# Mixture-of-experts layer with a domain adapter on one core: index records for SyncE, a hold on GpSimd's output operations, one power per layernorm

## The chip, the cores and the metric

The kernel runs on one core of a Trainium2 chip. The metric is the device time of one launch in microseconds (us), the median of several runs. TensorE does the matmuls, VectorE, ScalarE and GpSimd the elementwise work, and SyncE (SP) issues most of the DMAs.

## What is computed

128 sequences of 64 tokens with 256 features each go through two layers. Each sequence has an expert out of 8 and a domain out of 16.

```python
h = gelu(x @ Wi[e] + bi[e]); o = h @ Wo[e] + bo[e]        # 256 -> 1024 -> 256, e = itok_B_0_7
y = layernorm(o + x, 1e-12) * gamma[e] + beta[e]
a = gelu(y @ down_W.T + down_b)                            # 256 -> 64
a = where(valid, a @ expert_W[d].T + expert_b[d], a) + domain_emb[d]   # d = itok_B_0_15
out = layernorm(a @ up_W.T + up_b + y, 1e-5) * ln_gamma + ln_beta
```

## The kernel before

**Tiles.** A tile is two sequences of the same expert: 128 tokens. A sort on VectorE, TensorE and GpSimd in the first 15 us assigns the sequences to 136 slots, two per tile, so that there are 68 tiles, some with empty slots. It writes the indices that address the DMAs and the weights into the one row `idx`: for each slot the source (`IDX_SRC`) and the destination (`IDX_DST`), per tile the expert, for each of 64 weight chunks its place in HBM (`IDX_CHUNK`), and four numbers per step for TensorE. The engines load them into registers as they need them (`index`, `indices`).

**Precision.** Every f32 operand of a large product is split into a high and a low f16 part. ScalarE writes the high part (`x_hi`, `h_hi`, W's half), VectorE the low one (`x_lo` L723, `h_lo` L764, W's other half L727) as scaled value minus high part, and TensorE does three products (L918 to L920, L926 to L928).

**Steps.** The program is a software pipeline. Step i does, on the engines at the same time: the first product of tile i and, behind it, the second product of tile i-1 in eight parts j (TensorE), the first layernorm of tile i-2 (`r1`, `bn_stats`, `bn_aggr`, `z1`), the transposition of z1 between the fourth and fifth part of the second product (L959), the adapter's down product for tile i-3 and its up product and second layernorm for tile i-4, and the output of tile i-5. 73 steps in all; steps 0 to 7 are written out, the middle is a loop whose body holds 4 steps (8 on ScalarE and VectorE), the end is written out again. In the steps with weights one more weight chunk of 128 x 512 is loaded, split and stored, for a later expert.

**Every engine has its own queue in program order**, and engines meet at semaphores: `pe.wait_ge(z1_done, i - 1)` before the transposes, for example. What is written first on an engine runs first; a waiting instruction blocks everything behind it.

**VectorE's step:** r1 (L774, the product plus x, out of PSUM), its bn_stats (L777), r2 into yg (L783, out of PSUM), its bn_stats (L786), first bn_aggr (L788), low part of the adapter's activation `a1s` (L794), second bn_aggr (L797), the second half of h_lo for tile i-1, z1 (L805), y (L812), x_lo, the low part of a chunk, the first half of h_lo for tile i. `mv` holds mean and variance of both layernorms, `rs` their power -1/2.

**GpSimd's step:** for tile i-5 y times ln_gamma (L466) and plus ln_beta (L468); z1 times gamma into yg (L474); then one power for both layernorms of the step:

```python
pool.tensor_tensor(rs[:, both], mv[:, both, 1], neg_half[:, both], ALU.pow).then_inc(rs_done, 1)   # L484
```

and three small copies (L488, L494, L454) which gather gamma, the selection and the bias for ScalarE and TensorE.

**SP's step:** the chunk's index and the chunk for step i+2 (L253, L338), the sources of tiles i to i+2 and the transposed x of tile i+2 (L258, L322), the wait for `y_done`, the two destinations and two output DMAs (L258, L372), and x in its natural layout for tile i (L330). `x_T` and `y` have two buffers each.

Of the kernel before, what the change touches and what calls it, by code (L numbers as in the profile page):

```python
# [26 lines left out]
IDX_SRC, IDX_DST = 0, SLOTS  # L27

IDX_EXP = 2 * SLOTS + 3
IDX_CHUNK = IDX_EXP + TILES + 2  # L30

IDX_PE = IDX_CHUNK + CHUNKS
IDX_LEN = IDX_PE + 4 * STEPS


def build(nc, t):
# [4 lines left out]
    with ctx:  # L41
# [136 lines left out]
        CHUNK_READY, SRC_READY, TILE_READY, ALL_READY = 1, 2, 3, 4  # L178
# [45 lines left out]
        rs_done = sem("rs_done")  # L224
# [78 lines left out]
        def _(sp):  # L303
# [13 lines left out]

            def load_turned(b, i, parity):
# [23 lines left out]
            def load_first(chunks, of):  # L342
                for c, m in zip(chunks, of):
                    sp.dma_start(first_stage[m], t["w"][bass.ds(c * P, P), :]).then_inc(first_in[m], 16)

            chunks = indices(sp, IDX_CHUNK, FIRST_CHUNKS // 2, CHUNKS - 1)
            load_first([chunks[m] for m in FIRST_ORDER[:4]], FIRST_ORDER[:4])
            load_first(indices(sp, IDX_CHUNK + FIRST_CHUNKS // 2, FIRST_CHUNKS // 2, CHUNKS - 1), FIRST_ORDER[4:])
            sp.wait_ge(idx_ready, SRC_READY)
            b = [indices(sp, 2 * i + IDX_SRC, 2, B - 1) for i in range(2)]  # L350
            load_turned(b[1], 1, 1)
            for j in range(AHEAD):
                load_later(j, j % SLOTS_W)
# [6 lines left out]
            def step(i, parity, four, weights):  # L360
                if weights:
                    load_later(i + AHEAD, weights[2])

                if exists(i):
                    b = indices(sp, 2 * i + IDX_SRC, 6 if exists(i + 2) else 2, B - 1)
                if exists(i + 2):
                    load_turned(b[4:6], i + 2, parity)
                if exists(i - 5):
                    sp.wait_ge(y_done, i - 4)
                    to = indices(sp, 2 * i + (IDX_DST - 10), 2, SLOTS - 1)  # L370
                    for n in range(2):
# [705 lines left out]
```

## Time and profile before

| | us |
|---|---|
| median of 3 runs | 537.85 (537.72 to 538.39) |
| profiled execution | 537.86 |
| its span, first to last instruction | 535.9 |
| TensorE busy | 493.2 (92%) |
| VectorE busy | 423.7 (79%) |
| ScalarE busy | 381.8 (71%) |
| GpSimd busy | 315.0 (59%) |
| SP among the chain that ended last | 37% |

The span is the time between the first and last instruction of the core; a little lies around it. Busy shares are coverage: matmuls overlap each other, so TensorE's 92% does not say that 8% could be had. TensorE's granted clock is 1.00 of full speed in the whole tile loop. PE is TensorE, PEld its weight loads, DVE VectorE, ACT ScalarE, POOL GpSimd; a q behind it is the engine's own queue of instructions that compute nothing, such as issuing a DMA.

### The profile page before, as it was taken

The page shows a single profiled execution, that of the slowest core. Times are in us where ns is not written, and L with a number is a line of the kernel's source. Part 1 is how long each engine was busy: PE and PEld are TensorE (multiplying, and loading weights), DVE is VectorE, ACT ScalarE, POOL GpSimd, SP SyncE. Part 2 cuts the span into 40 slices and gives each one's busy share as a digit, 9 for nine tenths or more (in the row PEclk, how much of TensorE's full clock was granted, in tenths as well). Part 3 has the DMA queues.
Part 4 walks back from the last instruction along what each step waited for, and adds up shares of the span by engine and source line. Part 5 has one row for each costly group of instructions (what it writes and reads, how often), then busy time and mean ns, then how long its engine had stood idle before and what let it go on. Part 6 is the DMA issues. An engine that isn't in the chain of part 4 may idle for free.

```text
span 535.9 us, 19427 instructions
## 1 busy us (share of the span) xinstructions
PE 493.2 (92%) x5778; PEld 432.0 (81%) x5779; DVE 423.7 (79%) x935; ACT 381.8 (71%) x1099; POOL 315.0 (59%) x521
## 2 busy tenths in 40 slices
PE   5699999999999999999989999999999999999962
PEld 3489988888888878888878888888878888888951
DVE  6677888888888888788888888887888877677762
ACT  2688777787877777777778777787777876677741
POOL 5043666666656566565665566655666655555554
PEclk9799999999999999999999999999999999999995
DMA  4734333333333333323333333333333222222111
GB/s 115 245 95 103 87 91 94 79 91 89 93 93 80 87 92 89 92 78 90 91 90 91 84 91 87 90 90 87 87 88 89 63 64 58 61 62 56 46 32 29
DMA packets 70256, 45.83 MB, mean 86 GB/s; under 512 B 43969, under 2 KB 61778, under 8 KB 70098
## 3 DMA queue, kind: packets, MB, share of 16 engines
q1 hardware_dynamic: 69200, 45.25, 31.5%
q8 instruction: 15, 0.25, 0.2%
q10 hardware_dynamic: 1026, 0.21, 0.2%
q14 instruction: 15, 0.12, 0.1%
HBM read 36.51 MB, written 8.91 MB: 85 GB/s over the span
## 4 chain that ended last, share of the span: by engine, by line
SPq 37%; PE 35%; issue 11%; DVE 6%; POOL 4%; DMA 3%; ACT 2%; POOLq 1%; DVEq 0%; ACTq 0%
SPq L258 9%; SPq L322 8%; SPq L372 7%; SPq L330 7%; PE p_h L918 5%; PE p_h L919 4%; PE p_h L920 4%; PE p_o L928 4%; PE p_o L926 4%; PE p_o L927 4%; SPq L338 3%; PE p_d L937 2%; DMA x_T<-in_xT 2%; POOL rs L484 2%; PE p_t L959 2%
## 5 line engine op out<-in xcount | busy, mean ns | idle before, releaser
L918 PE MATMUL p_h<-x_hi,W 128*128 128x128 f16 x1088 | 194.0, 220 | 5.6 <-issue 5.3
L919 PE MATMUL p_h<-x_lo,W 128*128 128x128 f16 x1088 | 193.4, 220 | 0.0
L920 PE MATMUL p_h<-x_hi,W 128*128 128x128 f16 x1088 | 193.3, 220 | 0.0
L484 POOL TENSOR_TENSOR rs<-mv,neg_half 128x2 f32<-128x2 f32 (+1 forms) x70 | 67.6, 966 | 162.4 <-DVE mv L797 156.8
L581 ACT ACTIVATE h<-p_h,bi_tile 128x128 f32<-128x128 f32 x544 | 152.6, 362 | 0.4 <-PE p_h L920 0.4
L926 PE MATMUL p_o<-W,h_hi 128*128 x544 | 148.3, 273 | 0.0
L927 PE MATMUL p_o<-W,h_hi 128*128 x544 | 148.3, 273 | 0.0
L928 PE MATMUL p_o<-W,h_lo 128*128 x544 | 148.3, 273 | 0.0
L764 DVE SCALAR_TENSOR_TENSOR h_lo<-h,h_hi 128x512 f16<-128x512 f32 x136 | 124.5, 915 | 1.0 <-ACT h_hi L589 0.9
L918 PEld LDWEIGHTS p_h<-x_hi,W 128*128 x1088 | 106.7, 98 | 19.7 <-issue 18.3
L919 PEld LDWEIGHTS p_h<-x_lo,W 128*128 x1088 | 106.7, 98 | 1.5
L920 PEld LDWEIGHTS p_h<-x_hi,W 128*128 x1088 | 106.7, 98 | 0.0
L589 ACT ACTIVATE h_hi<-h 128x512 f16<-128x512 f32 x136 | 85.4, 628 | 2.2
L555 ACT ACTIVATE x_hi<-x_T 128x256 f16<-128x256 f32 x68 | 28.3, 416 | 72.5 <-DMA x_T<-in_xT 72.4
L474 POOL TENSOR_TENSOR yg<-z,g_t 128x256 f32<-128x256 f32 x68 | 73.2, 1076 | 2.5 <-DVE z L805 2.5
L468 POOL TENSOR_TENSOR y<-y,lnb 128x256 f32<-128x256 f32 x68 | 70.2, 1033 | 5.3
L466 POOL TENSOR_TENSOR y<-y,lng 128x256 f32<-128x256 f32 x68 | 56.6, 832 | 25.6 <-DVE y L812 25.6
L727 DVE SCALAR_TENSOR_TENSOR W<-stage,W 128x512 f32 (+1 forms) x56 | 66.5, 1187 | 0.1
L805 DVE TENSOR_SCALAR z<-r,mv,rs 128x256 f32<-128x256 f32 x68 | 32.2, 473 | 39.9 <-POOL rs L484 39.9
L621 ACT ACTIVATE yT<-p_t,gb_tile 128x128 f32<-128x128 f32 x136 | 54.8, 454 | 9.9 <-PE p_t L959 5.7
L928 PEld LDWEIGHTS p_o<-W,h_lo 128*128 128x128 f16 x544 | 53.2, 98 | 6.2
L927 PEld LDWEIGHTS p_o<-W,h_hi 128*128 128x128 f16 x544 | 53.2, 98 | 6.2
(153 smaller groups left out, 715.7 us busy)
## 6 DMA issues: line engine op xcount, KB each, us to landing
stage<-in_w SPq DMA_DIRECT2D x56, 256.0 KB, 2.6
x_nat<-in_x SPq DMA_DIRECT2D x136, 64.0 KB, 2.1
out<-y SPq DMA_DIRECT2D x136, 64.0 KB, 2.0
x_T<-in_xT SPq DMA_DIRECT2D x134, 64.0 KB, 2.2
W<-in_w SPq DMA_DIRECT2D x8, 256.0 KB, 4.1
g_t<-in_gamma SPq DMA_DIRECT2D x1, 1024.0 KB, 7.7
W<-in_expert_W SPq DMA_DIRECT2D x2, 128.0 KB, 3.0
upT<-in_up_W SPq DMA_DIRECT2D x2, 64.0 KB, 2.6
```

What stands on the lines that cost most here:

```text
L468: pool.tensor_tensor(last, last, lnb[:, :], ALU.add).then_inc(y_done, 1)
L474: pool.tensor_tensor(yg[:, 1 - parity, :], z1[:, :], g_t[:, bass.ds(e_third * D, D)], ALU.mult)\
L484: pool.tensor_tensor(rs[:, both], mv[:, both, 1], neg_half[:, both], ALU.pow).then_inc(rs_done, 1)
L581: ins = nc.scalar.activation(h[:, c, :], p_h[parity][:, c, :], ACT.Gelu, bias=bi_tile[:, parity, c:c + 1], scale=1.0 / (XS * WS))
L589: nc.scalar.activation(h_hi[:, parity, cols_h, :], h[:, cols_h, :], ACT.Copy, scale=HS)\
L764: v.scalar_tensor_tensor(h_lo[:, parity, cols_h, :], h[:, cols_h, :], HS, h_hi[:, parity, cols_h, :], ALU.mult, ALU.subtract).then_inc(hlo ...
L918: mm(p_h[parity][:, c, :], hi, x_hi[:, parity, k, :], start=(k == 0), stop=False)
L919: mm(p_h[parity][:, c, :], hi, x_lo[:, parity, k, :], start=False, stop=False)
L920: ins = mm(p_h[parity][:, c, :], lo, x_hi[:, parity, k, :], start=False, stop=(k == KD - 1))
L926: mm(p_o[:, 0:D], h_hi[:, parity, j, :], hi, start=False, stop=False)
L927: mm(p_o[:, 0:D], h_hi[:, parity, j, :], lo, start=False, stop=False)
L928: return mm(p_o[:, 0:D], h_lo[:, parity, j, :], hi, start=False, stop=(j == KI - 1))
```

## The change

Five edits, in the diff's own order of things:

- **Index records.** `idx` gets six numbers per step for SP side by side: sources of tiles i and i+2 and destinations of tile i-5. SP reads them with one load at the head of its step, ahead of the wait for y. Chunks are addressed as the expert's first chunk plus a constant, so one index is loaded per expert, that is per eight steps, and SP's loop body holds 8 steps instead of 4. The sort writes the sources twice (one copy more on VectorE), and ScalarE, which issues the first x_T, waits for the first of the copies only.
- **Hold.** GpSimd's first output operation waits also for `hlo_half`, the first half of h_lo in VectorE's step i-1, which is the last operation of that step.
- **One power per layernorm**, each behind its own bn_aggr and with its own semaphore.
- **The first bn_aggr ahead of the second bn_stats** on VectorE.
- **y behind x_lo** on VectorE, where it stood ahead of it.

```diff
-IDX_SRC, IDX_DST = 0, SLOTS
+IDX_SP = 0
+IDX_PE = IDX_SP + 6 * STEPS
+IDX_EXP = IDX_PE + 4 * STEPS + 3
...
-            def load_later(j, slot_n):
+            def load_later(j, expert, m, slot_n):
                 if not isinstance(j, int) or j >= SLOTS_W:
                     sp.wait_ge(w_lo, j - (SLOTS_W - 1))
-                c = index(sp, IDX_CHUNK + FIRST_CHUNKS + j, CHUNKS - 1)
-                sp.dma_start(stage[:, slot_n, :], t["w"][bass.ds(c * P, P), :]).then_inc(w_in[slot_n], 16)
+                sp.dma_start(stage[:, slot_n, :], t["w"][bass.ds((expert + m) * P, P), :]).then_inc(w_in[slot_n], 16)
...
                 if weights:
-                    load_later(i + AHEAD, weights[2])
-                if exists(i):
-                    b = indices(sp, 2 * i + IDX_SRC, 6 if exists(i + 2) else 2, B - 1)
+                    if weights[0] == 0:
+                        expert[0] = first_chunk(weights[1])
+                    load_later(i + AHEAD, expert[0], weights[0], weights[2])
+                if exists(i + 2) or exists(i - 5):
+                    b = indices(sp, 6 * i + IDX_SP, 6, SLOTS - 1)
                 if exists(i + 2):
-                    load_turned(b[4:6], i + 2, parity)
+                    load_turned(inside(b[2:4]), i + 2, parity)
                 if exists(i - 5):
                     sp.wait_ge(y_done, i - 4)
-                    to = indices(sp, 2 * i + (IDX_DST - 10), 2, SLOTS - 1)
...
-            run(sp, step, SLOTS_W, AHEAD)
+            run(sp, step, NCH, AHEAD)
...
                     pool.wait_ge(z2_done, i - 4)
+                    pool.wait_ge(hlo_half, 2 * min(i, TILES) - 1 if isinstance(i, int) else 2 * i - 1)
...
-                    if exists(i - 2):
-                        pool.wait_ge(mv1_done, i - 1)
-                    if exists(i - 4):
-                        pool.wait_ge(mv2_done, i - 3)
-                    pool.tensor_tensor(rs[:, both], mv[:, both, 1], neg_half[:, both], ALU.pow).then_inc(rs_done, 1)
+                if exists(i - 2):
+                    pool.wait_ge(mv1_done, i - 1)
+                    pool.tensor_tensor(rs[:, 0:1], mv[:, 0, 1:2], neg_half[:, 0:1], ALU.pow).then_inc(rs1_done, 1)
+                if exists(i - 4):
+                    pool.wait_ge(mv2_done, i - 3)
+                    pool.tensor_tensor(rs[:, 1:2], mv[:, 1, 1:2], neg_half[:, 0:1], ALU.pow).then_inc(rs2_done, 1)
...
-            v.tensor_copy(idx[:, IDX_SRC:IDX_DST], p_t[0:1, 0:SLOTS]).then_inc(idx_ready, 1)
+            v.tensor_copy(sp_idx[:, 0:TILES, 0:2], src).then_inc(idx_ready, 1)
+            v.tensor_copy(sp_idx[:, 0:TILES - 2, 2:4], src[:, 2:TILES, :]).then_inc(idx_ready, 1)
...
-                    dve.wait_ge(r2_done, i - 3)
-                    v.bn_stats(st2[:, 0:6], yg[:, parity, :]).then_inc(st2_done, 1)
                 if exists(i - 2):
                     v.bn_aggr(mv[:, 0, :], st1[:, :]).then_inc(mv1_done, 1)
                 if exists(i - 4):
+                    dve.wait_ge(r2_done, i - 3)
+                    v.bn_stats(st2[:, 0:6], yg[:, parity, :]).then_inc(st2_done, 1)
                     dve.wait_ge(st2_done, i - 3)
...
-                    dve.wait_ge(rs_done, i - 1)
+                    dve.wait_ge(rs1_done, i - 1)
```

**Where instructions move.** VectorE, one step of the tile loop, before (st and mv stand for both layernorms: r1's come first):

```order
L774 SCALAR_TENSOR_TENSOR r<-p_o,x_nat 128x256
L777 BN_STATS st<-r 128x6
L783 SCALAR_TENSOR_TENSOR yg<-p_u,yg 128x256
L786 BN_STATS st<-yg 128x6
L788 BN_AGGR mv<-st 128x2
L794 SCALAR_TENSOR_TENSOR a1s<-a,a1s 64x2x64
L797 BN_AGGR mv<-st 128x2
L764 SCALAR_TENSOR_TENSOR h_lo<-h,h_hi 128x512
L805 TENSOR_SCALAR z<-r,mv,rs 128x256
L812 TENSOR_SCALAR y<-yg,mv,rs 128x256
L723 SCALAR_TENSOR_TENSOR x_lo<-x_T,x_hi 128x256
L727 SCALAR_TENSOR_TENSOR W<-stage,W 128x2x256
```

and in the change:

```order
L785 SCALAR_TENSOR_TENSOR r<-p_o,x_nat 128x256
L788 BN_STATS st<-r 128x6
L794 SCALAR_TENSOR_TENSOR yg<-p_u,yg 128x256
L797 BN_AGGR mv<-st 128x2
L800 BN_STATS st<-yg 128x6
L805 SCALAR_TENSOR_TENSOR a1s<-a,a1s 64x2x64
L808 BN_AGGR mv<-st 128x2
L775 SCALAR_TENSOR_TENSOR h_lo<-h,h_hi 128x512
L816 TENSOR_SCALAR z<-r,mv,rs 128x256
L733 SCALAR_TENSOR_TENSOR x_lo<-x_T,x_hi 128x256
L825 TENSOR_SCALAR y<-yg,mv,rs 128x256
L737 SCALAR_TENSOR_TENSOR W<-stage,W 128x2x256
```

The first bn_aggr stands one place earlier, ahead of yg's bn_stats, and y one place later, behind x_lo.

GpSimd, one step of the tile loop with what each instruction waits for, before:

```order
L258 TENSOR_LOAD idx
L466 TENSOR_TENSOR y<-y,lng 128x256 [waits z2_done]
L468 TENSOR_TENSOR y<-y,lnb 128x256 [waits zg_done]
L474 ISA [waits z1_done]
L474 TENSOR_TENSOR yg<-z,g_t 128x256
L484 TENSOR_TENSOR rs<-mv,neg_half 128x2 [waits mv2_done,mv1_done]
L488 ISA [waits yT_done]
L488 COPY gb_tile<-gb_c 128x4
L494 COPY sel_tile<-sel 128x128 [waits up_done]
L454 ISA [waits gelu_half]
L454 COPY bi_tile<-bi_c 128x8
```

and in the change:

```order
L262 TENSOR_LOAD idx
L475 TENSOR_TENSOR y<-y,lng 128x256 [waits hlo_half,z2_done]
L477 TENSOR_TENSOR y<-y,lnb 128x256 [waits zg_done]
L483 ISA [waits z1_done]
L483 TENSOR_TENSOR yg<-z,g_t 128x256
L488 TENSOR_TENSOR rs<-mv,neg_half 128x1 [waits mv1_done]
L492 TENSOR_TENSOR rs<-mv,neg_half 128x1 [waits mv2_done]
L496 ISA [waits yT_done]
L496 COPY gb_tile<-gb_c 128x4
L502 COPY sel_tile<-sel 128x128 [waits up_done]
L461 ISA [waits gelu_half]
L461 COPY bi_tile<-bi_c 128x8
```

The first output operation has a second wait, with yg and the powers in the queue behind it; the power of the first layernorm waits for mv1_done alone.

SP, from the weight chunk to the first output DMA of a step in the loop, before:

```order
L253 TENSOR_LOAD idx [waits w_lo]
L338 ISA
L338 DMA stage<-in_w 128x512
L258 TENSOR_LOAD idx
L322 ISA [waits x_split]
L322 DMA x_T<-in_xT 128x2x64
L322 ISA
L322 DMA x_T<-in_xT 128x2x64
L258 TENSOR_LOAD idx [waits y_done]
L372 ISA
L372 DMA out<-y 64x256
```

and in the change, a step that is not the first of its expert:

```order
L345 ISA [waits w_lo]
L345 DMA stage<-in_w 128x512
L262 ISA
L262 TENSOR_LOAD idx
L253 REGISTER_ALU
L330 ISA [waits x_split]
L330 DMA x_T<-in_xT 128x2x64
L330 ISA
L330 DMA x_T<-in_xT 128x2x64
L377 REGISTER_ALU
L379 ISA [waits y_done]
```

The load of the chunk's index and that of the destinations are gone, and the wait for y stands directly at the output DMA.

## Rows read from the trace of the kernel before

**Rows 1.** The head of the page.

```profile
span 535.9 us, 19427 instructions
```

**Rows 2.** Waits, 35 to 511 us: who waited for whom, total us, times, longest.

```profile
ACT x_hi L555 <- DMA x_T<-in_xT: 71.4, 46, 2.2
...
DVE z L805 <- POOL rs L484: 38.1, 65, 0.6
...
PEld p_t L959 <- DVE z L805: 28.5, 66, 1.0
...
PEld p_h L918 <- issue: 17.3, 57, 0.8
```

**Rows 3.** TensorE in the timeline, step 66: start, duration, engine, line.

```profile
503.53 0.27 PE L928 MATMUL p_o<-W,h_lo 128*128 x1
...
503.75 0.20 PEld L959 LDWEIGHTS p_t<-ident,z 128*128 128x128 f32 x2 [0.23 <-DVE z L805]
```

**Rows 4.** Timeline of step 67: from the down product to z1.

```profile
506.92 0.66 PE L937 MATMUL p_d<-yT,downT 128*128 128x128 f32 x4
...
507.62 0.37 ACT L605 ACTIVATE a<-p_d,downb 128x128 f32<-128x128 f32 x1 [2.07 <-PE p_d L937]
...
508.02 0.31 ACT L608 ACTIVATE a1s<-a 128x128 f16<-128x128 f32 x1
...
508.43 0.29 DVE L794 SCALAR_TENSOR_TENSOR a1s<-a,a1s 64x128 f16<-64x128 f32 x1 [0.94 <-ACT a1s L608]
...
508.75 0.20 DVE L797 BATCH_NORM_AGGREGATE mv<-st 128x2 f32<-128x9 f32 x1
...
508.86 0.65 DVE L764 SCALAR_TENSOR_TENSOR h_lo<-h,h_hi 128x512 f16<-128x512 f32 x1
...
509.09 0.98 POOL L484 TENSOR_TENSOR rs<-mv,neg_half 128x2 f32<-128x2 f32 x1 [2.33 <-DVE mv L797]
...
510.10 0.48 DVE L805 TENSOR_SCALAR z<-r,mv,rs 128x256 f32<-128x256 f32 x1 [0.59 <-POOL rs L484]
```

**Rows 5.** The chain of waits on SP in the middle of the loop: start, duration, line.

```profile
254.45 0.28 SPq L253
...
257.94 0.47 SPq L258
...
261.43 0.29 SPq L253
```

**Rows 6.** Timeline of VectorE and GpSimd in step 7.

```profile
67.06 0.84 POOL L466 TENSOR_TENSOR y<-y,lng 128x256 f32<-128x256 f32 x1 [0.36 <-DVE y L812]
...
67.24 1.21 DVE L727 SCALAR_TENSOR_TENSOR W<-stage,W 128x512 f16<-128x512 f32 x1
...
67.98 1.06 POOL L468 TENSOR_TENSOR y<-y,lnb 128x256 f32<-128x256 f32 x1
...
68.38 1.21 DVE L764 SCALAR_TENSOR_TENSOR h_lo<-h,h_hi 128x512 f16<-128x512 f32 x1
...
69.01 1.17 POOL L474 TENSOR_TENSOR yg<-z,g_t 128x256 f32<-128x256 f32 x1
...
69.52 0.41 DVE L774 SCALAR_TENSOR_TENSOR r<-p_o,x_nat 128x256 f32<-128x256 f32 x1
```

**Rows 7.** The same operations later in the timeline, GpSimd uncontended.

```profile
505.54 0.42 DVE L774 SCALAR_TENSOR_TENSOR r<-p_o,x_nat 128x256 f32<-128x256 f32 x1
...
506.04 0.72 POOL L474 TENSOR_TENSOR yg<-z,g_t 128x256 f32<-128x256 f32 x1
...
526.99 0.56 POOL L484 TENSOR_TENSOR rs<-mv,neg_half 128x1 f32<-128x1 f32 x1 [2.08 <-DVE mv L797]
528.08 0.72 POOL L466 TENSOR_TENSOR y<-y,lng 128x256 f32<-128x256 f32 x1 [0.53 <-DVE y L812]
```

**Rows 8.** Timeline of VectorE, the last z1.

```profile
521.89 0.41 DVE L805 TENSOR_SCALAR z<-r,mv,rs 128x256 f32<-128x256 f32 x1 [1.17 <-POOL rs L484]
```

**Rows 9.** Timeline of VectorE, the copy of the source indices.

```profile
9.44 0.29 DVE L698 CAST idx<-p_t 1x136 int32<-1x136 f32 x1
```

More of the change, by code:

```diff
@@ L223, in build @@
         mv1_done = sem("mv1_done")
-        rs_done = sem("rs_done")
+        rs1_done = sem("rs1_done")
+        rs2_done = sem("rs2_done")
         z1_done = sem("z1_done")
@@ L316, in _, with inside @@
                 sp.dma_start(downb[half, :], t["down_b"].rearrange("(p a) -> p a", a=1)).then_inc(adapter_in, 16)
+            def inside(b):
+                return [nc.s_assert_within(r, 0, B - 1, skip_runtime_bounds_check_because="the sorting clips every index")
+                        for r in b]
             def load_turned(b, i, parity):
@@ L331, in load_natural, with first_chunk @@
                       .then_inc(xnat_in[parity], 16)
-            def load_later(j, slot_n):
+            def load_later(j, expert, m, slot_n):
                 if not isinstance(j, int) or j >= SLOTS_W:
                     sp.wait_ge(w_lo, j - (SLOTS_W - 1))
-                c = index(sp, IDX_CHUNK + FIRST_CHUNKS + j, CHUNKS - 1)
-                sp.dma_start(stage[:, slot_n, :], t["w"][bass.ds(c * P, P), :]).then_inc(w_in[slot_n], 16)
+                sp.dma_start(stage[:, slot_n, :], t["w"][bass.ds((expert + m) * P, P), :]).then_inc(w_in[slot_n], 16)
+            def first_chunk(place_n):
+                return index(sp, IDX_CHUNK + place_n, CHUNKS - NCH)
             sp.wait_ge(idx_ready, CHUNK_READY)
[L342 to L348, printed above, removed]
+            expert = first_chunk(0)
+            for m in FIRST_ORDER:
+                sp.dma_start(first_stage[m], t["w"][bass.ds((expert + m) * P, P), :]).then_inc(first_in[m], 16)
             sp.wait_ge(idx_ready, SRC_READY)
-            b = [indices(sp, 2 * i + IDX_SRC, 2, B - 1) for i in range(2)]
-            load_turned(b[1], 1, 1)
+            load_turned(indices(sp, IDX_SP + 6, 2, B - 1), 1, 1)
+            expert = [first_chunk(1)]
             for j in range(AHEAD):
-                load_later(j, j % SLOTS_W)
+                load_later(j, expert[0], j, j % SLOTS_W)
             sp.dma_start(g_t[:, :], t["gamma"].partition_broadcast(P)).then_inc(g_in, 16)
@@ L539, in _ @@
             nc.scalar.copy(b_s[:, :], ph_flat[0][:, 0:D]).then_inc(b_ready, 1)
-            act.wait_ge(idx_ready, SRC_READY)
-            b = indices(act, IDX_SRC, 2, B - 1)
+            act.wait_ge(idx_ready, FIRST_READY)
+            b = indices(act, IDX_SP, 2, B - 1)
             for n in range(2):
@@ L682, in _ @@
             link(v.tensor_reduce(ord_f[:, :], cube[0:1, :, :], AX.X, ALU.add))
-            v.scalar_tensor_tensor(idx[:, IDX_CHUNK:IDX_PE].rearrange("a (e c) -> a e c", c=NCH), wide(ord_f[:, :]),
-                                   float(NCH), rows(iota_e[0:1, :], E0), ALU.mult, ALU.add).then_inc(idx_ready, 1)
+            v.tensor_scalar(idx[:, IDX_CHUNK:IDX_LEN], ord_f[:, :], float(NCH), None, ALU.mult).then_inc(idx_ready, 1)
             link(v.tensor_tensor(cube[:, :, :], ahead[:, :, :], rows(two_pairs[:, :], E0), ALU.mult))
@@ L756, in _ @@
             link(v.scalar_tensor_tensor(row, row, float(B), empty, ALU.add, ALU.mult))
-            v.tensor_tensor(idx[:, IDX_DST:2 * SLOTS], row, p_u[0:1, 2 * SLOTS:3 * SLOTS], ALU.add)\
+            v.tensor_tensor(sp_idx[:, 5:TILES + 5, 4:6], row.rearrange("a (t n) -> a t n", n=2),
+                            p_u[0:1, 2 * SLOTS:3 * SLOTS].rearrange("a (t n) -> a t n", n=2), ALU.add)\
                 .then_inc(idx_ready, 1)
@@ L806, in step @@
                         .then_inc(z1_done, 1)
+                if exists(i + 1):
+                    low_x(i + 1, 1 - parity)
                 if exists(i - 4):
-                    dve.wait_ge(rs_done, i - 1)
+                    dve.wait_ge(rs2_done, i - 3)
                     if not isinstance(i, int) or i >= 6:
```

18 lines of the change are left out of this document (7 added, 11 removed).

## The prediction

> **What bounds the kernel now.** I read the page's head first, then the waits, then the timeline of one step of the tile loop, then the chain of waits. The page gives the span, 535.9 us [rows 1]; the profiled execution took 537.86 us, so 2.0 us lie around it, and it stands within 0.01 us of the median, 537.85.
>
> One step handles one tile. TensorE is the engine that does not rest: the waits between 35 and 511 us show it idle only before the transposes of z1 (PEld 28.5 us, 66 times) and at the first product of a step (17.3 us, "issue") [rows 2]. The first is a stall on VectorE's z1 in **every** step. The second comes mostly from the loop's way back every four steps; TensorE's code is unchanged, so it stays.
>
> What a stall costs is read from the smallest one. The last L928 before it starts at 503.53, the transposes at 503.75, where these matmuls follow each other at 0.11 [rows 3]: the row says 0.23 idle, but only 0.11 to 0.12 are lost. So of 28.5 us, 66 x 0.12 = 7.9 are no loss, and **20.6 us** are lost, 7.9 as the standing 0.12 per step, 12.7 as the surplus of the late steps.
>
> Why z1 is late: within a step a chain begins and ends on TensorE [rows 4]. The down product (506.92) releases ScalarE's gelu (507.62) and a1s (508.02), then on VectorE the low part (508.43), the second bn_aggr (508.75) and h_lo (508.86). The one power waits for both bn_aggr and runs 509.09 to 510.07; z1 idles 0.59 for it, although its own bn_aggr had long been done, and starts at 510.10.
>
> Why some steps are worse: SP is full. Between two equal places of its queue, the load of a chunk index at 254.45 and the next at 261.43, lie 6.98 us with no wait in them [rows 5], so x_T arrives late, and ScalarE idles 71.4 us in 46 steps for it [rows 2]. Its a1s, and the chain above, start later there.
>
> And VectorE is full too, since two of its largest operations last 1.21 us each, W's low part and the first h_lo (67.24, 68.38), while the second h_lo, equally large, lasts 0.65 [rows 4, 6]. Beside the slow ones run GpSimd's L466, L468 and L474 (67.06, 67.98, 69.01), themselves at 0.84, 1.06 and 1.17 instead of 0.72 [rows 6, 7]. A step now lasts 7.27 us on average: VectorE's r1 stands at 69.52 and, 60 steps later, at 505.54 [rows 6, 7].
>
> **The change, part by part.**
>
> *A power per layernorm, bn_aggr ahead of the second bn_stats.* GpSimd can make rs for z1 once the first bn_aggr is there, before the chain through a1s ends. z1 then follows the second h_lo directly: 508.86 + 0.65 = 509.51, with 0.03 of hand-over at 509.54 instead of 510.10, 0.56 earlier. The transposes could start 0.12 before 510.64 (not in the rows: it is 0.06 behind the end of z1, 510.10 + 0.48); z1 ends at 510.02. That leaves 0.4 to 0.5 us to spare, and the standing stall goes: 7.9 us. The power of one column costs 0.56 where two columns took 0.98 [rows 4, 7]; two of them are 0.1 us more GpSimd work per step, hidden in its waiting.
>
> *GpSimd's output operations held* until VectorE has done the first h_lo. Removed: the company of 1.21 us operations. I price W's low part and h_lo at 0.65, VectorE work falling by 2 x 0.56 = 1.1 us a step. That is hidden gain, spare time and not a term. Added: L466, L468, L474 now run beside r1, bn_stats and r2. r1 lasts 0.41 at 69.52 beside L474 (69.01 to 70.18), and L474 lasts 0.72 at 506.04 beside bn_stats and r2 [rows 6, 7], so I take 0.72 each there. Behind the held operations on GpSimd stand yg, the power for z1, then the second power. They end 3 x 0.72 + 0.56 = 2.7 us plus some 0.3 of hand-overs after VectorE's step end. z1 comes later than that: VectorE needs five operations at about 0.42, then must wait for ScalarE's a1s, which TensorE's phase fixes. L468 now ends (69.04) 0.5 us before the next r1 [rows 6]; held, it ends 1.5 behind it, and VectorE is 1.1 earlier: y comes some 0.9 us later, and the output DMAs queue behind that on SP.
>
> The Trainium skill, "SBUF — State Buffer", section "SBUF: two separate sides", says that the pair of ports common to VectorE and GpSimd is an exclusive lock, taken for a whole instruction, by a VectorE operation with two SBUF inputs against a GpSimd one that reads SBUF. The trace agrees: 1.21 us where 0.65 are needed. The rule also speaks against the change, as the first rival below.
>
> *SP's records.* In a step the two separate loads go, 0.28 for the chunk and 0.47 for the destinations [rows 5], with their dispatch some 1.1 us; one load per eight steps returns. SP's 6.98 us become about 5.9, under the 6.8 that I expect of a step. x_T of tile i+2 then leaves one tile early enough that ScalarE finds it. With it and a lighter VectorE the surplus of the late steps goes: 12.7 us. From below: if SP still held x_T back, nothing of this.
>
> *Order of x_lo and y:* swapped, equal lengths, nobody waits for y within the step; 0.
>
> *The end.* In the last two steps with z1 it waited 0.59 and 1.17 us [rows 4, 8], and everything after it is one serial chain: 0.56 + 1.14 = 1.7 us. The last destinations are now loaded before the wait for y, 0.5 us [rows 5]. *The start:* the sort is one serial chain on VectorE; a second copy of the kind of the one at 9.44, 0.29 long there [rows 9], costs 0.3 us at most. Fewer index loads before the first chunks are hidden: ScalarE needs TensorE's table first.
>
> **Sum:** 537.86 - 7.9 - 12.7 - 1.7 - 0.5 + 0.3 = 515.4 us. What remains is TensorE's own pace: steps of about 6.75 to 6.85 us and 0.5 more every fourth.
>
> **The rivals.**
>
> 1. *The stall survives by a little.* The second power reads SBUF, starts as h_lo ends and runs 0.56 beside z1; if it holds z1 back until about 509.93 to 510.07, z1 ends at 510.4 or 510.5 and the standing 0.12 remains, while the surplus goes: 515.4 + 7.9 = **523.3**. For it: z1 is 0.48 instead of 0.41 beside small GpSimd copies [rows 4, 8]. Against: the first of those times still gives the transposes in time. This is what the Trainium skill's lock would do, by the section named above. Chance 0.18.
>
> 2. *SP stays the bound.* The later y_done stops SP, and x_nat and the next x_T queue behind it. y comes 0.9 us later, 1.1 us of work is saved, so it is close; the surplus would stay: 515.4 + 12.7 = **528.1**. Chance 0.09.
>
> 3. *Slower: contention only moves, and the hold closes a loop.* Hold, lng, lnb, yg, power, z1, x_lo, y, low part, first h_lo, next hold is a closed ring over two engines. With all at the contended lengths it is 0.84 + 1.06 + 1.17 + 0.56 + 0.48 + 2 x 0.41 + 2 x 1.21 = 7.35, with 0.5 of hand-overs 7.85, 0.58 more than today's 7.27, 60 times: 537.9 + 35 = **573**. It decides as soon as the ring exceeds 7.27. At the free lengths it is 3 x 0.72 + 0.56 + 0.48 + 0.82 + 2 x 0.65 + 0.5 = 5.8. Chance 0.04: r1 and bn_stats ran undisturbed beside L474.
>
> 4. *The hold does not do what it says*, since other GpSimd work falls beside the two large operations: VectorE keeps 1.21 us, the early z1 still pays. This lies between my forecast and rival 1 and needs no own case.
>
> **How the numbers follow.** The forecast has 0.69, the rivals 0.18, 0.09 and 0.04. The time is the likeliest one's, 515.4. Below, 512: the late x_T also costs ScalarE in the first steps, which no term holds, up to some 3 us. Above, the range takes in rival 1 and part of the way to rival 2: 526; rivals 2 and 3 are left out. A measurement tells 0.2%, about 1 us, from no change. Faster by more: all but rival 3 and a remainder, 0.95; within 0.2%: 0.01; slower: 0.04.
>
> **What would show it.** Right: in the waits, PEld before the transposes near 1 us instead of 28.5 in this stretch; ScalarE's wait for x_T nearly gone; VectorE's W low part and both h_lo near 0.65; GpSimd's L466, L468, L474 near 0.72; VectorE's wait for the power gone, its wait for a1s longer; SP with waits for y in each step. Wrong: z1 idle for a power, r1 or bn_stats longer than 0.45, x_hi still waiting for its DMA in most steps, or a new wait of TensorE at down or up.

## The result and the profile after

| | before | the change |
|---|---|---|
| median of 4 runs | 538.06 us (537.72 to 538.39) | 499.01 us (498.85 to 499.39) |
| profiled execution | 537.86 us | 498.85 us |
| its span | 535.9 us | 497.1 us |

The ratio is 0.9275, 95% interval 0.9259 to 0.9291. The gain is 39 us where 22.5 were forecast: the direction was right, and the time lies below the whole range.

The head of the page after, the busy times of the engines (share of the span), and the shares of the chain that ended last:

```profile
span 497.1 us, 19258 instructions
...
PE 473.9 (95%) x5778; PEld 438.7 (88%) x5779; DVE 355.6 (72%) x936; ACT 373.8 (75%) x1099; POOL 358.6 (72%) x587
...
PE 93%; DVE 3%; POOL 1%; issue 1%; DMA 0%; ACT 0%; POOLq 0%; DVEq 0%
```

TensorE is now nearly the whole chain. The waits of the changed kernel between 35 and 470 us (who waited for whom, total us, times, longest), its costliest first:

```profile
ACT a L613 <- PE p_d L948: 84.3, 64, 2.0
POOL rs L492 <- DVE mv L808: 71.2, 63, 1.5
DVE a1s L805 <- ACT a1s L616: 65.0, 64, 1.1
DVE r L785 <- PE p_o L939: 40.4, 62, 1.3
...
PEld p_h L929 <- issue: 2.8, 13, 0.3
```

Beside [rows 2]: ScalarE's 71.4 us for x_T and TensorE's 28.5 for z1 are gone, VectorE's 38.1 for the power is 0.5. And TensorE's "issue" idle at the first product of a step is 2.8 us in 13 places instead of 17.3 in 57. That last line the prediction had said would stay.

Where SP now waits (whole span):

```profile
SPq L379 <- POOL y L477: 33.0, 40, 2.9
```

VectorE of the changed kernel in one ordinary step of the loop (start, duration, engine, line):

```profile
225.20 0.20 DVE L808 BATCH_NORM_AGGREGATE mv<-st 128x2 f32<-128x9 f32 x1
225.31 0.65 DVE L775 SCALAR_TENSOR_TENSOR h_lo<-h,h_hi 128x512 f16<-128x512 f32 x1
225.88 0.41 DVE L816 TENSOR_SCALAR z<-r,mv,rs 128x256 f32<-128x256 f32 x1
...
226.86 0.68 DVE L737 SCALAR_TENSOR_TENSOR W<-stage,W 128x512 f32 x1
227.46 0.68 DVE L775 SCALAR_TENSOR_TENSOR h_lo<-h,h_hi 128x512 f16<-128x512 f32 x1
228.69 0.42 DVE L785 SCALAR_TENSOR_TENSOR r<-p_o,x_nat 128x256 f32<-128x256 f32 x1 [0.55 <-PE p_o L939]
```

z1 (L816) follows h_lo without the 0.59 of [rows 4], and the two operations of 1.21 in [rows 6] last 0.68. The Trainium skill, "SBUF — State Buffer", section "SBUF: two separate sides", ties the long durations to GpSimd's company; the trace agrees in so far as GpSimd in the same step has its three operations of 128x256 only after them:

```profile
228.39 0.73 POOL L475 TENSOR_TENSOR y<-y,lng 128x256 f32<-128x256 f32 x1
229.19 0.72 POOL L477 TENSOR_TENSOR y<-y,lnb 128x256 f32<-128x256 f32 x1
229.88 0.72 POOL L483 TENSOR_TENSOR yg<-z,g_t 128x256 f32<-128x256 f32 x1
```

They last 0.72 to 0.73 instead of 0.84, 1.06 and 1.17. But another operation of GpSimd now stands beside VectorE's y, W's low part and first h_lo, the small copy of the selection. Before, and after:

```profile
226.12 0.28 POOL L494 COPY sel_tile<-sel 128x128 f16 x1
```

```profile
226.61 1.68 POOL L502 COPY sel_tile<-sel 128x128 f16 x1
```

So the company has in part moved to an operation that nobody waits for; it is one reason for GpSimd's higher busy share (72% after, 59% before).

TensorE around the same z1, which ends at 226.29, and around the way back of its loop one step later:

```profile
226.85 0.25 PEld L970 LDWEIGHTS p_t<-ident,z 128*128 128x128 f32 x2
...
228.38 0.10 PEld L929 LDWEIGHTS p_h<-x_hi,W 128*128 x1
...
235.25 0.10 PEld L929 LDWEIGHTS p_h<-x_hi,W 128*128 x1 [0.21 <-issue]
```

z1 is there 0.56 us before the transposes' weights are loaded and 0.67 before their first matmul. No gap stands before the next step's first product (its weights at 228.38, its matmul at 228.49). At the way back the row says 0.21 idle; weights usually run one place, 0.11, ahead of their matmul, so the matmul itself is 0.10 late. Below, "first product" is the start of that matmul.

**Where the 39 us come from.** I followed the start of each step's first product in both timelines. From that of step 5 to that of step 67, 62 steps later, before takes 54.46 to 505.34 = 450.9 us and after 54.14 to 470.04 = 415.9 us: 7.27 and 6.71 a step. An undisturbed step after is 6.67, so 62 of them are 413.5. The rest, 37.4 and 2.4 us, split by its place on TensorE:

| excess over 6.67 per step, us | before | after | forecast to go |
|---|---|---|---|
| idle before the transposes | 19.9 | 0 | 20.6 |
| first product, every fourth step (way back) | 7.6 | 1.3 | 0 |
| first product, other steps | 3.3 | 0 | 0 |
| products just behind the transposes | 3.4 | 0 | 0 |
| elsewhere | 3.2 | 1.1 | 0 |

35.0 us are gained there, 3.5 in the tail (30.6 to 27.1 us) and 0.3 at the start. The question for the experiments: why did places clear that nobody had touched, TensorE's own first products above all?

### The profile page after: what moved, and what is told of

Read it like the earlier page. It is cut to its first block, busy times and chain, and to the rows that moved or that the text cites. A ratio compares the mean times of both kernels' runs of the same rounds, so it can differ in the third digit from the quotient of the medians.

```text
span 497.1 us, 19258 instructions
## 1 busy us (share of the span) xinstructions
PE 473.9 (95%) x5778; PEld 438.7 (88%) x5779; DVE 355.6 (72%) x936; ACT 373.8 (75%) x1099; POOL 358.6 (72%) x587
## 4 chain that ended last, share of the span: by engine, by line
PE 93%; DVE 3%; POOL 1%; issue 1%; DMA 0%; ACT 0%; POOLq 0%; DVEq 0%
PE p_h L929 13%; PE p_h L931 12%; PE p_h L930 12%; PE p_o L939 12%; PE p_o L938 12%; PE p_o L937 12%; PE p_d L948 7%; PE p_u L962 6%; PE p_t L970 3%; PE p_u L958 2%; PE p_o L1028 1%; PE p_h L872 1%; DVE W L737 1%; POOL y L475 0%; PE p_t L872 0%
## 5 line engine op out<-in xcount | busy, mean ns | idle before, releaser
L492 POOL TENSOR_TENSOR rs<-mv,neg_half 128x1 f32<-128x1 f32 x68 | 59.7, 878 | 74.2 <-DVE mv L808 74.2
L613 ACT ACTIVATE a<-p_d,downb 128x128 f32<-128x128 f32 x68 | 25.0, 367 | 90.0 <-PE p_d L948 90.0
L775 DVE SCALAR_TENSOR_TENSOR h_lo<-h,h_hi 128x512 f16<-128x512 f32 x136 | 91.1, 670 | 1.4 <-ACT h_hi L597 1.4
L502 POOL COPY sel_tile<-sel 128x128 f16 (+1 forms) x68 | 81.0, 1191 | 2.0 <-issue 2.0
L805 DVE SCALAR_TENSOR_TENSOR a1s<-a,a1s 64x128 f16<-64x128 f32 x68 | 19.7, 289 | 66.5 <-ACT a1s L616 66.4
L475 POOL TENSOR_TENSOR y<-y,lng 128x256 f32<-128x256 f32 x68 | 49.3, 726 | 20.5 <-DVE h_lo L775 18.7
L785 DVE SCALAR_TENSOR_TENSOR r<-p_o,x_nat 128x256 f32<-128x256 f32 x68 | 28.8, 424 | 44.2 <-PE p_o L939 44.1
L938 PEld LDWEIGHTS p_o<-W,h_hi 128*128 128x128 f16 x544 | 53.2, 98 | 6.2
L937 PEld LDWEIGHTS p_o<-W,h_hi 128*128 128x128 f16 x544 | 53.2, 98 | 4.7
```

The lines of the kernel that those rows point to most:

```text
L492: pool.tensor_tensor(rs[:, 1:2], mv[:, 1, 1:2], neg_half[:, 0:1], ALU.pow).then_inc(rs2_done, 1)
L502: pool.tensor_copy(sel_tile[:, four, :].rearrange("p (n s) -> p n s", n=2), sel[:, bass.ds(2 * i, 2)].unsqueeze(2).to_broadcast([P, 2, S]))\
L775: v.scalar_tensor_tensor(h_lo[:, parity, cols_h, :], h[:, cols_h, :], HS, h_hi[:, parity, cols_h, :], ALU.mult, ALU.subtract).then_inc(hlo ...
L937: mm(p_o[:, 0:D], h_hi[:, parity, j, :], hi, start=False, stop=False)
L938: mm(p_o[:, 0:D], h_hi[:, parity, j, :], lo, start=False, stop=False)
```

## The experiments

Two groups: which part of the change carries the gain (e1 to e4, e11, e14), and why TensorE's first products followed z1 (the others). Ratios are against before on the same chip, with 95% intervals.

### Part by part

**e1, the change with SP's old index loads.**

```diff
-expert[0] = first_chunk(weights[1])      # one load per eight chunks
+c = index(sp, IDX_CHUNK + FIRST_CHUNKS + j, CHUNKS - 1)
+to = indices(sp, 2 * i + (IDX_DST - 10), 2, SLOTS - 1)
```

> The change with SP's index records as before. Theory: SP's queue needs 6.98 us a step again, more than TensorE's 6.67, so SP sets the pace, x_T is late and the transposes wait in part of the steps: 515 to 520 us. Rival: the records were not needed once z1 was early and VectorE light: 499 to 502 us.

528.48 us, ratio 0.9834 (0.9814 to 0.9854): a miss, too high. ScalarE waits for x_T 79.2 us in 48 steps between 35 and 480 us. The chain of waits of e1, SP's load of the chunk index (L254) in successive steps and its load of six source indices (L259) in three of them:

```profile
252.69 0.28 SPq L254
...
259.66 0.29 SPq L254
...
260.62 1.27 SPq L259
...
267.60 0.28 SPq L254
...
268.55 0.73 SPq L259
...
274.61 0.27 SPq L254
...
275.68 1.27 SPq L259
...
282.29 0.28 SPq L254
```

The steps are 6.97, 7.94, 7.01 and 7.68 long, 7.40 on average. The six indices take 0.73 in one step and 1.27 in the next, by turns, and the way back of SP's loop falls into the second of the four. The same holds before: SP's steps in the middle of the loop average 7.40 there too, and so do TensorE's from step 28 to 52, in both kernels (after: 6.72). [rows 5] show one of the short steps, 6.98. So in the steps with weights SP allows no better than 7.40, early z1 or not; the 9.2 us that e1 gains lie outside that stretch. Seen from the other side, the records are worth some 30 us where the powers are in (528.48 against 499.01), against 12.7 where they are not (e4).

**e2, the change with one joined power and bn_aggr behind the second bn_stats.**

```diff
-pool.wait_ge(mv1_done, i - 1); pool.tensor_tensor(rs[:, 0:1], ...).then_inc(rs1_done, 1)
-pool.wait_ge(mv2_done, i - 3); pool.tensor_tensor(rs[:, 1:2], ...).then_inc(rs2_done, 1)
+pool.wait_ge(mv1_done, i - 1); pool.wait_ge(mv2_done, i - 3)
+pool.tensor_tensor(rs[:, both], mv[:, both, 1], neg_half[:, both], ALU.pow).then_inc(rs_done, 1)
```

> The change with one power for both layernorms and the first bn_aggr behind the second bn_stats, as before. Theory: the transposes wait some 0.12 us in every step again (7.5 us in all), and each wait of TensorE's queue costs more than its idle time, since behind it the 0.06 at the next product and the loop's way back of 0.5 every four steps are exposed: 512 to 515 us, with a gap of about 0.5 before the first product of every fourth step. Rival: the stall costs its idle time alone: 506 to 507 us, gap at the way back 0.1.

525.17 us, ratio 0.9764 (0.9747 to 0.9780): a miss, 10 us above the upper expectation. The powers cost or give 26 us, although the stall before the transposes that comes back is only a few tenths. Its waits from 35 to 480 us:

```profile
DVE z L815 <- POOL rs L491: 36.5, 62, 0.6
PEld p_h L928 <- issue: 16.6, 57, 0.8
PEld p_t L969 <- DVE z L815: 15.8, 62, 0.5
```

With z1's wait for the power the "issue" line is back at 16.6 in 57 places, and the gap of about 0.5 at the way back came as expected. This is the line that made me look at what TensorE's queue does behind z1.

**e3, the change without the hold**, and **e11, before with only the hold.**

```diff
-pool.wait_ge(hlo_half, 2 * min(i, TILES) - 1 if isinstance(i, int) else 2 * i - 1)
```

(e3; e11 adds this line to before.)

> The change without the hold on GpSimd's output operations. Theory: VectorE's W low part and first h_lo go back to 1.21 us, 1.1 us a step, which the wait of 1.0 us for a1s takes up: 499 to 501 us. Rival: the hold carries the gain (VectorE was full): 505 us or more.

> The kernel before with the hold alone. Theory: SP and the one power set the pace, a lighter VectorE buys nothing: 536 to 540 us. Rival: VectorE was full and late steps catch up: 532 us or less.

e3: 499.43 us, 0.9293 (0.9276 to 0.9311). e11: 537.48 us, 0.9998 (0.9986 to 1.0009). Both times as expected: the hold is worth nothing that can be told, with or without the rest, as it was priced. The reason given for e3 did not come, though: without the hold only 8 of VectorE's 108 operations of 128x512 between 95 and 335 us last 1.2 us, the others 0.65 to 0.69, as GpSimd, busy with its long copy until then, mostly comes to its output operations after them anyway (read from the rows, not tested). The test of the company is e11, where both large operations fall to 0.66 and 0.68 on average and VectorE's busy time between 95 and 335 us from 202.0 to 169.6 us, for nothing: VectorE was not what bound the kernel before.

**e4, before with the records alone.** Its diff is that of the change in SP's program and the index table.

> The kernel before with SP's index records alone. Theory: x_T is in time, the late steps' surplus goes (12.7 us), the standing wait before the transposes and the exposed way back stay: 522 to 526 us. Rival: y and z1 hold the pace, not SP: 534 us or more.

524.95 us, ratio 0.9765 (0.9749 to 0.9781), and the surplus of the late steps is gone: 537.68 - 524.95 = 12.7 us against the term of 12.7. (In the timelines the idle time before the transposes falls by 11.5, from 19.9 to 8.4; the rest is elsewhere, so the agreement to the tenth is luck.) ScalarE's wait for x_T is no longer among the costliest. What is left is z1 late in every step. TensorE of e4 around one such z1, and the next first product:

```profile
228.62 0.48 DVE L813 TENSOR_SCALAR z<-r,mv,rs 128x256 f32<-128x256 f32 x1 [0.59 <-POOL rs L489]
...
229.16 0.20 PEld L967 LDWEIGHTS p_t<-ident,z 128*128 128x128 f32 x2 [0.24 <-DVE z L813]
...
230.79 0.10 PEld L926 LDWEIGHTS p_h<-x_hi,W 128*128 x1 [0.16 <-issue]
```

z1 ends at 229.10, the first product starts at 230.79: 1.69 us. And in between, on TensorE's queue, the load of the next step's four indices into registers (durations min/median/max, start):

```profile
L261 PEldq TENSOR_LOAD <-idx x1: 997/997/997, 229.3 to 229.3; - x1
```

It starts 0.24 behind z1's end, lasts 1.00, and the first product follows 0.45 behind its end. In that 0.45 the queue runs three register operations of L915, the addresses of the first product's weights:

```profile
L915 PEldq FUSED_REGOPS  x3: 60/79/79, 230.4 to 230.7; - x3
```

At a way back of the same kernel z1 ends at 243.02 and the matmul starts 2.20 later. The loop's compare-and-branch, which has register operations on both sides, stands ahead of the load:

```profile
L283 PEldq COMPARE_BRANCH  x1: 213/213/213, 243.3 to 243.3; - x1
```

```profile
L261 PEldq TENSOR_LOAD <-idx x1: 1007/1007/1007, 243.8 to 243.8; - x1
```

So the load starts 0.75 behind z1's end instead of 0.24: that is the 0.5 of the way back.

**e14, the change without the hold, bn_aggr late, y ahead of x_lo**: the records and two powers only.

```diff
-pool.wait_ge(hlo_half, 2 * min(i, TILES) - 1 if isinstance(i, int) else 2 * i - 1)
...
+v.bn_stats(st2[:, 0:6], yg[:, parity, :]).then_inc(st2_done, 1)
...
-v.bn_stats(st2[:, 0:6], yg[:, parity, :]).then_inc(st2_done, 1)
...
-low_x(i + 1, 1 - parity)
...
+low_x(i + 1, 1 - parity)
```

> The change without the hold, with the first bn_aggr behind the second bn_stats and y ahead of x_lo, as before: SP's records and two powers alone. Theory: nothing but these two carries the gain: 498.5 to 500.5 us. Rival: with GpSimd and VectorE in each other's way, the first power comes too late without the earlier bn_aggr: 503 us or more.

500.05 us, 0.9291 (0.9275 to 0.9306), as expected. The rest of the change is worth 1.0 us at most; the intervals overlap, and the 62 steps take 416.0 us as against 415.9, although a third of VectorE's operations of 128x512 last 1.2 us here.

So the records alone gain 12.7, all of the change but the records 9.2 (e1, 537.68 - 528.48), both 39: about 17 us appear only together. Two limits lay close to one another, SP at 7.40 in the steps with weights and z1's ring at 6.94, with its ways back 7.09 (TensorE's steps of e4 in the same stretch). Removing one shows the other. VectorE, with its operations of 1.21 and its wait for the power, needs less than either: an estimate from e4 is 6.8 (240 us between 95 and 335, less 10.7 in which it waits for ScalarE and TensorE, over 33.9 steps).

### Why the first products follow z1

**e5, e6, e7: the change with z1 delayed**, by unused operations put just ahead of it on VectorE.

```diff
+v.bn_stats(scr[:, 0:6], r1[:, :])                                  # e5, e6, e7
+v.bn_aggr(mv3[:, 2:4], st3[:, :]); v.bn_aggr(mv3[:, 4:6], st3[:, :])  # e6
+v.bn_stats(scr[:, 6:12], r1[:, :])                                 # e7
```

> The change with one extra bn_stats on VectorE before z1 (result unused), some 0.46 us later. z1 stays ready before the transposes (it ends 0.67 us ahead of them). Theory (TensorE's queue loses its lead only where it truly waits): 499 us as the change, steps of 6.67, way back 0.1. Rival (the pace depends on how long before its use z1 is signalled, or on VectorE's load): 505 us or more.

> The change with one bn_stats and two bn_aggr more before z1, some 0.7 us later: z1 is late by 0 to 0.15 us. Theory: even so small a wait in each step exposes all of it, the 0.06 behind the transposes, the 0.05 at the step's start and the way back of 0.45 every four steps: 517 to 526 us for 62 waits of at most 0.15 (9 us at most). Rival (cost is proportional to the wait): at most 508 us.

> The change with two extra bn_stats before z1, 0.92 us later: late by some 0.3 us. Theory: what e6 pays and the additional idle time, about 0.2 us more in each of 62 steps: 12 us over e6, 533 to 540 us, with a gap at the way back no larger than in e6. Rival (the exposed part grows with the wait): over 545 us.

| | median us | ratio | z1 ends against the transposes | gap at the way back | z1's end to the first product: ordinary, way back |
|---|---|---|---|---|---|
| the change | 499.01 | 0.9275 | 0.67 ahead | 0.10 | 2.20, 2.31 |
| e5 | 502.38 | 0.9332 (0.9316 to 0.9348) | 0.35 ahead | 0.28 to 0.32 | 1.88, 2.17 |
| e6 | 506.63 | 0.9412 (0.9396 to 0.9428) | 0.21 ahead | 0.46 | 1.74, 2.20 |
| e7 | 517.88 | 0.9622 (0.9606 to 0.9638) | 0.03 late | 0.56 | 1.69, 2.20 |
| e2, e4 | 525.17, 524.95 | | late | 0.5 | 1.69, 2.20 |

The delays came out at 0.32, 0.46 and 0.70 us, less than the 0.46, 0.7 and 0.92 meant, so z1 of e6 was never late, as its theory wanted. e5 missed both numbers, e6 met the rival's, e7 missed both. My theory at that time, that the queue loses its lead only where it truly has to wait, would have kept e5 at 499: it fell. What holds through all rows is the last column: as z1 gets later the distance to the next first product (a median over the loop's steps) shrinks to **1.69 us in an ordinary step and 2.17 to 2.20 over the way back, and no further**. In all of them but the change the index load starts 0.24 behind z1's end in an ordinary step, whether z1 is in time for the transposes or not. The waits of the three, in the same order, show TensorE's first product growing:

```profile
PEld p_h L934 <- issue: 5.3, 13, 0.4
```

```profile
PEld p_h L936 <- issue: 8.2, 17, 0.6
```

```profile
PEld p_h L935 <- issue: 16.3, 57, 0.7
```

So a z1 that is in time for the transposes can still be too late for the next step. The way back needs 2.2 us from z1's end; the transposes and the products behind them take 1.64 where nothing holds them up (the steps that are written out, and e15 below). In an ordinary step the queue's 1.69 is thus only 0.05 above what the matmuls need by themselves, at the way back 0.56.

**e8, the change, and e10, e4, with eight steps between TensorE's ways back instead of four; e9, the same for SP in e1.**

```diff
-run(pe, step)                      # e8, e10
+run(pe, step, NCH)
-run(sp, step, SLOTS_W, AHEAD)      # e9
+run(sp, step, NCH, AHEAD)
```

> The change with TensorE's loop body at 8 steps instead of 4. Theory: the way back is hidden but for 0.1 us, so half as many ways back save 0.7 us at most: 498 to 499 us. Rival: the longer body costs fetches of its own and the time rises by over 1 us.

> As e4 (the kernel before with the records alone), but TensorE's loop body 8 steps long. Theory: there the lead is gone and each way back costs 0.45 us; 7 fewer save 3.1 us, where the same edit on the change saved 0.6: 521.5 to 522.5 us. Rival: the gap of every fourth step has another source (a VectorE or GpSimd way back) and stays: 524.5 to 525.5 us.

> As e1 (the change with SP's old index loads), but SP's loop body 8 steps long. Theory: SP sets the pace there, 6.98 us a step and about 1 us more at each of its ways back every four steps, 7.2 on average; with half as many ways back 7.1, some 6 us less over 49 steps: 521 to 525 us. Rival: SP's way back is hidden, and e1's time comes from something else: 527.5 to 529.5 us.

498.44 (0.9256, 0.9241 to 0.9272), 522.47 (0.9713, 0.9692 to 0.9735) and 524.88 us (0.9775, 0.9748 to 0.9801), all in the range expected. Half the ways back are worth 0.6 us where z1 is early and 2.5 where it is late; half of SP's are worth 3.6 where SP is the limit. So before, TensorE's ways back cost what z1 made them cost. SP's cost less than e9's theory had it, 3.6 us instead of some 6: in the trace eight of its steps take 58.5 us instead of 59.2, 0.7 a way back and not 1.

**e12, e8 with z1 ahead of the second h_lo.**

```diff
-if exists(i - 1): split_h(i - 1, 1 - parity, 1)   # stood ahead of z1
+if exists(i - 1): split_h(i - 1, 1 - parity, 1)   # behind it
```

> The change with TensorE's loop body at 8 steps, and on VectorE z1 ahead of the second h_lo instead of behind it, so that the queue has more lead: z1 is signalled 0.6 us earlier. Theory: the way back's last 0.1 us is hidden too, 0.6 us for the body and 0.7 at most for the lead: 497.3 to 498.4 us. Rival: h_lo, which the second product needs right behind the transposes, becomes the wait: 502 us or more.

498.08 us, 0.9265 (0.9245 to 0.9286), as expected. z1 is 1.28 us early and gives nothing that can be told from e8. The traces say why: TensorE's index load stands 0.29 us ahead of the transposes in an ordinary step of the change, of e8 and of e12 alike, however early z1 is. For one step of the change, whose transposes start at 226.96:

```profile
L262 PEldq TENSOR_LOAD <-idx x1: 1002/1002/1002, 226.7 to 226.7; - x1
```

So with z1 early it is the queue's own progress that sets the load's start, and z1 no longer; over the way back, which needs 0.5 more, 0.10 of it stay uncovered. What holds the queue there no run shows.

**e13, e4 with the transposes two blocks of products later.**

```diff
-UP_AT, DOWN_AT, TR_AT = 0, 2, 4
+UP_AT, DOWN_AT, TR_AT = 0, 2, 6
```

> As e4 (the kernel before with the records alone, one power, z1 late), but the transposes stand before the seventh part of the second product instead of before the fifth, 0.65 us later in TensorE's program. Theory: z1 is then ahead of its wait and the queue has six products fewer to pass from there, so the stall, the 0.06 behind it and the 0.05 at a step's start vanish though z1 is as late as ever; only the way back keeps a part of its gap, 0.2 to 0.4: 502 to 507 us, ordinary steps 6.67 to 6.72. Rival (the exposed parts come from somewhere else, such as GpSimd's or VectorE's timing): only the stall of 0.12 a step goes, 516 to 518 us, with gaps of 0.5 at the way back.

521.86 us, 0.9699 (0.9683 to 0.9715): both expectations missed. TensorE's idle before the transposes is gone, and with it the delay of the products just behind them, yet only 3 us come of it, because the gap moved to the first product: its "issue" line rose from 16.6 us (e4) to 26.6. VectorE and TensorE's weight loads of one of its steps, from the timeline, and the index load of that step:

```profile
249.13 0.47 DVE L813 TENSOR_SCALAR z<-r,mv,rs 128x256 f32<-128x256 f32 x1 [0.59 <-POOL rs L489]
...
250.01 0.25 PEld L967 LDWEIGHTS p_t<-ident,z 128*128 128x128 f32 x2
...
251.25 0.10 PEld L926 LDWEIGHTS p_h<-x_hi,W 128*128 x1 [0.37 <-issue]
```

```profile
L261 PEldq TENSOR_LOAD <-idx x1: 998/998/998, 249.8 to 249.8; - x1
```

z1 ends at 249.60; the index load starts at 249.8, before the transposes run (250.01), and the first product comes 1.65 us behind z1. TensorE's queue had met z1's wait well ahead of the matmuls, and stood at it.

**e15, e4 with the next step's index load issued ahead of z1's wait, in three steps of four** (not across the way back); **e16, both e13 and e15; e17, e16 with eight steps between ways back; e18, the change with e17's load and eight steps.**

```diff
+if j == TR_AT and not LAST[0]:
+    loaded[0] = four_of(i + 1)          # ahead of the wait for z1
...
-there, here, *domains = [... indices(pe, 4 * i + IDX_PE, 4, DOMAIN_TOP) ...]
+there, here, *domains = loaded[0] if loaded[0] is not None else four_of(i)
```

> As e4 (the kernel before with the records alone, z1 late), but TensorE loads the four indices of the next step ahead of its wait for z1 instead of at the next step's start, in three steps of four (not over the loop's way back). Theory: the load of 1.00 us leaves the path from z1 to the next step's first product; what stays of a regular step is the stall of 0.12 and the 0.06 behind it, 6.85 to 6.88 instead of 6.95, and the gap of 0.05 at the start goes; the way back stays at 0.5: 519 to 522 us. Rival (another item behind z1 sets the next step's start): 524 us or more, gap at the start unchanged.

> As e13 (records alone, transposes two parts later, z1 late), with the load ahead of the wait in three steps of four. Theory: e13's gap of 0.18 to 0.25 at the start of a regular step vanishes, steps of 6.67 to 6.72, the way back keeps 0.65 to 0.8: 46 steps by 0.22 are 10 us: 509 to 513 us. Rival: 518 us or more.

> As e16 with TensorE's loop body at 8 steps. Theory: seven ways back and their loads fewer, 0.7 us each: 5 us less than e16, 504 to 508 us, though VectorE's z1 is as late as in the kernel before. Rival: as e16.

> The change with the load ahead and TensorE's loop body at 8 steps. Theory: with z1 early the load was hidden, so nothing is left to gain but the ways back, 0.6 to 1.0 us: 498 to 498.5 us. Rival: the load took TensorE's queue something there too: 496 us or less.

e15: 521.40 us, 0.9686 (0.9668 to 0.9703), as expected. The first product of one of its steps, whose z1 ends at 228.82, in the timeline, and the load:

```profile
230.35 0.10 PEld L931 LDWEIGHTS p_h<-x_hi,W 128*128 x1
```

```profile
L261 PEldq TENSOR_LOAD <-idx x1: 1008/1008/1008, 227.1 to 227.1; - x1
```

The load starts 1.7 us before z1 is ready, the first matmul follows z1's end by 1.64, and the gap before it is gone; the "issue" line falls from 16.6 us in 57 places to 9.3 in 15, the ways back alone. e16: 518.49 us, 0.9643 (0.9627 to 0.9659), above the expectation of 509 to 513 and in the range of the rival, 518 or more: the ordinary first products have no gap, but a way back costs 1.13 us (median), since z1 to first product is 2.12 there and the matmuls behind the transposes, two parts fewer, fill only about 1.0 of it. e17: 511.53 us, 0.9515 (0.9498 to 0.9531), also above its expectation, 504 to 508, though 7.0 below e16. That z1 still stops the queue at these ways back is seen; that the remainder of both misses is VectorE, which brings z1 at 5.53 us behind the step's start instead of e4's 5.26, with the 1.21 operations and z1's wait for the power (37.1 us in 63 steps of e16), is read from rows and was not tested by itself.

e18: 497.44 us (496.81 to 497.87), 0.9249 (0.9233 to 0.9264). It has the lowest median of all, 1.6 us below the change and somewhat below the expectation of 498 to 498.5, but its interval overlaps those of the change, e8 and e12. Its 62 steps take 415.2 us, just as in e8 (the change: 415.9), so the load ahead gives nothing in the loop where z1 is early; the rest of the 1.6 lies in the start and the tail, and the start varies between 52.9 and 55.1 us among all these kernels.

## Why the prediction was right and wrong

**Right.** The standing stall and the surplus of the late steps, 20.6 us together, measured 19.9; the surplus alone, 12.7, measured 11.5 before the transposes in e4, whose time fell by 12.7. Both came from the causes named: the joined power (e2) and SP's queue (e1). The hold as hidden gain, nothing (e11, e3). VectorE's large operations fell to 0.65 to 0.68, r1 and bn_stats stayed at 0.42 and 0.43 beside GpSimd, SP now waits for y (in 40 steps, not in each), and VectorE waits longer for a1s, as "what would show it" listed.

**Wrong, the step that failed**: "TensorE's code is unchanged, so it stays", of the 17.3 us at the first product, and with it "what remains is TensorE's own pace: steps of about 6.75 to 6.85 us and 0.5 more every fourth". The step is 6.67 and the fourth costs 0.10. The code was unchanged, but what its queue had to do behind z1's wait was not free of z1: it stops there, then loads four indices in 1.00 us, and in the loop the first product comes 1.69 us behind z1, 2.20 over the way back. e13 shows this path by itself (1.65 us with the transposes out of the way), and e15 takes the load out of it. Before, z1 ended 5.24 us behind the step's start (510.58 against 505.34), which is locked to that start by the chain of [rows 4]. 5.24 + 1.69 = 6.93, where an ordinary step took 6.94 to 6.95: the ring itself was the step wherever SP was not slower, and the 0.12 before the transposes was the part of it that showed as a stall. (In e7 z1 ends 5.16 behind the start, and the step is 6.87.) I priced the stall by its idle time and left its echo at the first product (6.3 + 3.3 us) and behind the transposes (3.4 us) to "own pace". With 2.1 elsewhere, unexplained, this is 15.1 us of the 16.5 missed in the profiled execution (515.4 against 498.85); the tail and the start bring 1.9, the stall -0.7.

That the echo behind the transposes (3.4 us) is the same mechanism is likely: of the three delayed kernels it comes back in e7 alone, the one with z1 late, and it is gone in e13, whose transposes never wait. No run isolates it.

**Mis-sized.** The tail: 1.7 + 0.5 - 0.3 = 1.9 forecast there and at the start, 3.8 to 3.9 measured. SP's step: 6.98 is one of its short steps, the average is 7.40, so it was SP that set the pace in the steps with weights, and the ring only elsewhere. With SP's queue lighter the ring stayed, 7.09 in the same steps (e4). The terms for the two could be added only because both causes went.

**Also off**: the second power lasts 0.89 beside h_lo instead of 0.56, and GpSimd's copy of the selection 1.68 instead of 0.28. Nobody waits for either in the loop. "VectorE is full too" did not hold: e11 freed it by a sixth and gained nothing.

**The rivals.** A little stall surviving, 523.3: its premise, z1 held back by the second power, did not come; z1 lasts 0.41. SP as bound, 528.1: it does not occur with the records, but e1, without them, is that case at 528.5 (though it was SP's own 7.40 that held it, not a late y). The closed ring, 573: its contention did move, to GpSimd's copy, but not to r1 and bn_stats, and no longer step came of it. A rival below the forecast was missing altogether: I never asked what TensorE would do with a z1 that is early, only what a late one costs.

**Still open**: why SP's load of six indices takes 0.73 and 1.27 by turns, what keeps TensorE's queue from getting more than 0.29 ahead of the transposes, and the 2.1 us elsewhere.

## What to carry to other kernels

A short idle gap before one instruction can be the visible part of a longer one: look at what the engine's queue has to do behind the same wait, register loads and a loop's way back above all, and price the distance from the awaited event to the next work of the step, not the gap. A place marked "issue" is a cost of the code only if it stays when the wait ahead of it in the queue is early; issue such loads ahead of the wait where registers allow. And where several limits stand within a few per cent of the step, part-by-part gains don't add: here 12.7 and 9.2 alone, 39 together, so count each limit's step over a whole turn of its loop, not between two places, before deciding which is the bound.

## What was unexpected in the hardware

TensorE's load of four indices takes 1.00 us, between 0.997 and 1.192 in 72 places; all index loads of the changed kernel by queue (durations in ns, min/median/max):

```profile
L262 SPq TENSOR_LOAD <-idx x74: 475/750/1308, 12.8 to 492.7; - x74
L262 PEldq TENSOR_LOAD <-idx x72: 997/1002/1192, 21.9 to 486.2; - x72
L262 POOLq TENSOR_LOAD <-idx x71: 562/1174/1281, 13.5 to 484.5; - x71
```

A load of one index takes SP 0.28 and of two 0.47 [rows 5], of six 0.73 or about 1.28, by turns from step to step. The Trainium skill, "DMA: Bandwidth & Descriptors", section "Latency and other measured facts", gives about 600 ns as the floor of such a load; SP's 0.28 and 0.47 lie below it, so the trace decides against it here. TensorE's 1.00 doesn't contradict it.

A loop's way back costs about 0.7 us of SP's queue (58.5 against 59.2 for eight steps, e9 and e1) and 0.5 of TensorE's (2.20 against 1.69), wherever the queue has no lead to hide it; with z1 0.67 us ahead of the transposes, 0.10 remain. TensorE's compare-and-branch alone takes 0.21, SP's 0.05 (medians of the change's 14 and 9).

GpSimd's copy of 128x128 f16 from SBUF to SBUF takes 0.28 us where VectorE leaves room and 1.68 beside VectorE's y, W's low part and first h_lo, six times as long, while these last 0.40, 0.68 and 0.68.
